# Routed feed-forward tiles: gated activations split into rounded halves ahead of the transpose, on one core

## What is computed

```python
sorted_x = xf[tok]                                   # tokens in the order of their experts
g = jax.lax.ragged_dot(sorted_x, gate_w, group_sizes)    # 512 -> 256
u = jax.lax.ragged_dot(sorted_x, up_w, group_sizes)      # 512 -> 256
h = jax.nn.silu(g) * u                               # gated activations
o = jax.lax.ragged_dot(h, down_w, group_sizes)       # 256 -> 512
o = o * w.reshape(-1)[order][:, None]
routed = jnp.zeros_like(xf).at[tok].add(o)
```

## Time and profile before

| | |
|---|---|
| median of three timed runs | 3971.14 us (3970.76 to 3972.11) |
| span of the profiled execution | 4018.9 us |
| TensorE matmuls busy | 3900.7 us, 97% of the span |
| ScalarE, VectorE, POOL busy | 1510.2, 1695.7, 1923.6 us |
| mean granted TensorE clock | 0.985 of full speed |
| routed stage, first matmul at | 1467.03 us |

### The profile page before, as it was taken

How to read it: one execution, slowest core, us unless ns; L and a number is a source line. 1 busy time by engine, 2 the same in 40 slices (tenths; PEclk the granted TensorE clock), 3 DMA queues, 4 the chain that set the end, 5 groups by cost and what they waited for, 6 DMA issues and landing times.

```text
span 4018.9 us, 92670 instructions
## 1 busy us (share of the span) xinstructions
PE 3900.7 (97%) x19160; PEld 3193.3 (79%) x19161; DVE 1695.7 (42%) x4076; ACT 1510.2 (38%) x3339; POOL 1923.6 (48%) x1598
## 2 busy tenths in 40 slices
PE   6999999999999969999999999999999999999998
PEld 5877777877777858888888888888888888888886
DVE  4655555555555533333333333333333333333343
ACT  3222222222222214444444444444444444444444
POOL 1353333333333425555555555555555555555554
PEclk7999999999999989999999999999999999999999
DMA  5121122121112126666676676767666776777776
GB/s 178 48 59 43 43 54 54 43 57 50 43 51 48 41 64 111 112 139 115 110 141 114 111 141 111 143 112 140 112 141 112 142 143 110 142 141 144 141 141 128
DMA packets 296940, 409.20 MB, mean 102 GB/s; under 512 B 116137, under 2 KB 151345, under 8 KB 296817
## 3 DMA queue, kind: packets, MB, share of 16 engines
q0 software_dynamic: 135872, 280.60, 37.8%
q1 hardware_dynamic: 160946, 127.03, 12.9%
HBM read 228.29 MB, written 179.19 MB: 101 GB/s over the span
## 4 chain that ended last, share of the span: by engine, by line
PE 62%; issue 1%; ACTq 0%; DMA 0%; ACT 0%; DVEq 0%; DVE 0%; SPq 0%; POOL 0%; POOLq 0%
PE bank L1229 37%; PE bank L1247 18%; PE bank L1220 4%; PE bank L1238 3%; ACTq L1325 0%; DMA raw_gu<-in_L_ffn_up_w_dram 0%; DVE w_dn_l L30 0%; DMA trow<-tile_table 0%; ACT w_gu_h L1317 0%; DVEq L1076 0%; POOL out_dram L1182 0%; SPq L1065 0%; ACTq L1065 0%; ACT x_h L1291 0%; ACT w_dn_h L1317 0%
## 5 line engine op out<-in xcount | busy, mean ns | idle before, releaser
L1182 POOL DMA_INDIRECT out_dram<-o_rows,to_row x532 | 862.1, 1620 | 970.0 <-issue 783.9
L422 POOL DMA_INDIRECT slot_list<-ent,pos x512 | 504.7, 986 | 874.8 <-PE bank L448 389.0
L1395 DVE TENSOR_TENSOR e_hf<-bank,e_sg 128x256 f32<-128x256 f32 x532 | 225.7, 424 | 1595.6 <-issue 808.6
L1229 PE MATMUL bank<-w_gu_h,x_h 128*128 x2128 | 842.9, 396 | 7.8 <-DVE x_l L30 5.1
L1229 PE MATMUL bank<-w_gu_l,x_h 128*128 x2128 | 840.9, 395 | 0.0
L1229 PE MATMUL bank<-w_gu_h,x_l 128*128 x2128 | 839.7, 395 | 0.0
L1166 POOL DMA_INDIRECT x_rows<-y_rows,from_row x536 | 537.6, 1003 | 215.1 <-issue 129.0
L1297 ACT ACTIVATE e_sg<-bank 128x256 f32<-128x256 f32 x532 | 204.3, 384 | 863.8 <-PE bank L1229 672.8
L1229 PEld LDWEIGHTS bank<-w_gu_h,x_h 128*128 128x128 f32 x2128 | 401.1, 188 | 109.8 <-issue 16.4
L1229 PEld LDWEIGHTS bank<-w_gu_h,x_l 128*128 128x128 f32 x2128 | 401.5, 189 | 94.2
L1229 PEld LDWEIGHTS bank<-w_gu_l,x_h 128*128 128x128 f32 x2128 | 401.2, 189 | 92.3
(11 more groups left out here) (244 smaller groups left out, 6022.8 us busy)
## 6 DMA issues: line engine op xcount, KB each, us to landing
xin<-in_x_dram SPq DMA_DIRECT2D x16, 1024.0 KB
y_rows<-yrow SPq DMA_DIRECT2D x64, 256.0 KB
stage_d<-in_x_dram SPq DMA_DIRECT2D x16, 1024.0 KB
out_dram<-stage_d SPq DMA_DIRECT2D x16, 1024.0 KB
raw_gu<-in_L_ffn_gate_w_dram SPq DMA_DIRECT2D x29, 512.0 KB
raw_gu<-in_L_ffn_up_w_dram SPq DMA_DIRECT2D x29, 512.0 KB
raw_d<-in_L_ffn_down_w_dram SPq DMA_DIRECT2D x29, 512.0 KB
lists<-slot_list SPq DMA_DIRECT2D x538, 1.0 KB
```

The lines of the kernel that those rows point to most:

```text
L422: nc.gpsimd.indirect_dma_start(slots, bass.IndirectOffsetOnAxis(ap=pos[v][:, t, k:k + 1], axis=0), ent[v][:, t, k, :], None).then_inc(scat ...
L1182: nc.gpsimd.indirect_dma_start(out, bass.IndirectOffsetOnAxis(ap=to_row[u][:].bitcast(U32), axis=0), og[u][:], None, compute_op=ALU.add).t ...
L1229: last = nc.tensor.matmul(b_gu[u % 2][:], xp[a][:, u % 2, k, :], wgu[b][:, bass.ds(place, 1), k, :].rearrange("p a n -> p (a n)"), start=( ...
L1395: nc.vector.tensor_tensor(hf[:, u % 2, :], b_gu[u % 2][:, H:2 * H], sg[:, u % 2, :], ALU.mult).then_inc(dve_gu, 1)
```

## The change

`e_hf` is no longer transposed itself. ScalarE rounds it into a high half `e_r_h` (`h_round`), VectorE subtracts that from `e_hf` into a low half `e_r_l` (`h_rest`), both of 128 x 256 in SBUF. `turn_h` transposes the two halves as float32r with `ident_r`, four transposes into all 512 columns of the bank, and waits for `dve_hr`, the low half. Behind it `h_high` still copies the first 256 columns to SBUF, and `h_low` copies the last 256 with a plain copy where it subtracted. In the order of the steps `h_round` stands between `x_high` and `h_high`, `h_rest` between `x_low` and `rows_from`. The wait for the turn of two tiles before moves from the product to the two new operations.

```diff
--- before.py
+++ after.py
@@ -1033,6 +1033,7 @@
             sg = sb("e_sg", [P, 2, H])
             hf = sb("e_hf", [P, 2, H])
             ident_r = sb("ident_r", [P, P], F32R)
+            hr = [sb("e_r_h", [P, 2, H], F32R), sb("e_r_l", [P, 2, H], F32R)]
             hp = [sb("e_h_h", [P, 2, KH, P], F32R), sb("e_h_l", [P, 2, KH, P], F32R)]
             og = [sb(f"o_rows{n}", [P, C]) for n in range(UN)]
 
@@ -1050,6 +1051,7 @@
             words, words_chain, ident_ok = sem("words"), sem("words_chain"), sem("ident_ok")
             pe_x, act_x, dve_x = sem("pe_x"), sem("act_x"), sem("dve_x")
             pe_gu, act_gu, dve_gu = sem("pe_gu"), sem("act_gu"), sem("dve_gu")
+            act_hr, dve_hr = sem("act_hr"), sem("dve_hr")
             pe_ht, act_ht, dve_ht = sem("pe_ht"), sem("act_ht"), sem("dve_ht")
             pe_do = sem("pe_do")
             act_do = sem("act_do")
@@ -1233,9 +1235,11 @@
 
                 def turn_h(j, u):
 
-                    pe.wait_ge(dve_gu, j + 1)
-                    for k in range(KH):
-                        last = nc.tensor.transpose(b_h[u % 2][:, k * P:(k + 1) * P], hf[:, u % 2, k * P:(k + 1) * P], ident[:])
+                    pe.wait_ge(dve_hr, j + 1)
+                    for a in range(2):
+                        for k in range(KH):
+                            last = nc.tensor.transpose(b_h[u % 2][:, a * H + k * P:a * H + (k + 1) * P].bitcast(F32R),
+                                                       hr[a][:, u % 2, k * P:(k + 1) * P], ident_r[:])
                     last.then_inc(pe_ht, 1)
 
                 def down(j, u, place):
@@ -1296,6 +1300,12 @@
                         act.wait_ge(dve_gu, j - 1)
                     nc.scalar.activation(sg[:, u % 2, :], b_gu[u % 2][:, 0:H], ACT.Silu).then_inc(act_gu, 1)
 
+                def h_round(j, u):
+                    act.wait_ge(dve_gu, j + 1)
+                    if not isinstance(j, int) or j >= 2:
+                        act.wait_ge(pe_ht, j - 1)
+                    nc.scalar.copy(hr[0][:, u % 2, :], hf[:, u % 2, :]).then_inc(act_hr, 1)
+
                 def h_high(j, u):
                     act.wait_ge(pe_ht, j + 1)
                     if not isinstance(j, int) or j >= 2:
@@ -1340,6 +1350,7 @@
                         start_weights(j + 2, turn.order(u + 2))
                     silu(j, u)
                     x_high(j + 2, (u + 2) % UN)
+                    h_round(j, u)
                     if not known or j >= 1:
                         h_high(j - 1, (u - 1) % UN)
                     with act.If(turn.first(u + 2) > 0):
@@ -1390,14 +1401,18 @@
 
                 def hidden(j, u):
                     dve.wait_ge(act_gu, j + 1)
+                    nc.vector.tensor_tensor(hf[:, u % 2, :], b_gu[u % 2][:, H:2 * H], sg[:, u % 2, :], ALU.mult).then_inc(dve_gu, 1)
+
+                def h_rest(j, u):
+                    dve.wait_ge(act_hr, j + 1)
                     if not isinstance(j, int) or j >= 2:
                         dve.wait_ge(pe_ht, j - 1)
-                    nc.vector.tensor_tensor(hf[:, u % 2, :], b_gu[u % 2][:, H:2 * H], sg[:, u % 2, :], ALU.mult).then_inc(dve_gu, 1)
+                    sub_exact(nc, hr[1][:, u % 2, :], hf[:, u % 2, :], hr[0][:, u % 2, :]).then_inc(dve_hr, 1)
 
                 def h_low(j, u):
                     dve.wait_ge(act_ht, j + 1)
-                    sub_exact(nc, hp[1][:, u % 2, :, :].rearrange("p k t -> p (k t)"), b_h[u % 2][:, 0:H],
-                              hp[0][:, u % 2, :, :].rearrange("p k t -> p (k t)")).then_inc(dve_ht, 1)
+                    nc.vector.tensor_copy(hp[1][:, u % 2, :, :].rearrange("p k t -> p (k t)"),
+                                          b_h[u % 2][:, H:2 * H]).then_inc(dve_ht, 1)
 
                 def weights_low(order, parts):
 
@@ -1416,6 +1431,7 @@
                         weights_low(turn.order(u + 1), (1, 2))
                     hidden(j, u)
                     x_low(j + 2, (u + 2) % UN)
+                    h_rest(j, u)
                     rows_from(j + 2 + UN, (u + 2) % UN, g + 2 if u >= UN - 2 else g + 1)
                     if not isinstance(j, int) or j >= 1:
                         h_low(j - 1, (u - 1) % UN)
```

## The result

The changed kernel takes 4075.74 us (median of 4 runs, 4070.72 to 4077.93); the kernel before, beside it, 3971.62 us. The ratio is 1.0259, with a 95% interval of 1.0246 to 1.0271: 104 us slower. The forecast was 4059 us, in a range of 3996 to 4096.

A forecast was written before the change was run, and what follows sets the result against it. TensorE was taken to bound the routed stage, 532 steps of 4.71 us. Turns +85 us and expert changes +3 us gave +88 us on the median 3971.14: 4059 us, range 3996 to 4096.

The forecast's parts named there:

- The bound: Routed stage: TensorE's chain of 532 steps of 4.71 us; other engines' work counts only where TensorE waits for it.
- The price of a turn: TensorE, each step: seven rounded turns at 0.083 us and an eighth at 0.11, +0.16 a step, +85 us.
- the block: TensorE's x and h turns in one routed step, forecast to take 0.69 us with eight rounded turns.
- e: Interval of the eighth rounded turn, with a down product's weight load under it: taken as 0.11 us, between 0.06 and 0.17.
- flat rate: Rival, TensorE turns: every rounded turn costs 0.073 us, +0.05 a step, +27 us, 3998 us; chance 0.11.
- short turns: Rival: the added four turns and the x turn ahead take 0.06 us or less, +0.02 a step, 3982 us; chance 0.05.
- faster: Rival: eight rounded turns fall under 0.53 us; at 0.06 each, -0.05 a step, -27 us, 3944 us; chance 0.03.
- What the chain would show: Changed profile: 8 turns of 0.69 to 0.75 us, a 4.87 us step, products unchanged at 2.79 and 1.40.
- ScalarE and VectorE in ordinary steps: Added 0.40 us on ScalarE and 0.42 on VectorE a step cost nothing; some 2 us of cover remain.
- The 48 us between the profiled span and the median: Profiled span 4018.9 us against median 3971.14, place unknown; the forecast difference was added to the median as it stood.
- Where an expert changes, the cover is thin: At 28 weight loads VectorE's +0.42 us lands on the chain: +0.1 us each, +3 us, ends -2 and +12.
- a sign of being wrong: Changed profile: more than a few us of the difference lying outside the four TensorE lines.

The follow-up runs named there:

- TensorE's part alone: Kernel before with four rounded turns of h in place of two plain ones, nothing added on ScalarE or VectorE: 4092.61 us beside 4007.89, ratio 1.0212.
- the first experiment: Kernel before with two rounded turns of h in place of the two plain ones, nothing else changed: 4008.03 us beside 4007.89, ratio 1.0001.
- The wait alone: Kernel before with ScalarE's wait for VectorE's product added, carried by an empty instruction, without the copy: ratio 1.0043, +16.9 us.
- both operations at the old speed: Kernel before with ScalarE's rounding copy and VectorE's subtraction added, results unused, the two plain turns kept: ratio 1.0057, +21.3 us.
- the copy alone: Kernel before with ScalarE's added copy of e_hf and its wait for VectorE's product, result unused: ratio 1.0055, +21.1 us.

## Why the prediction was right, and where it was not

**The bound.** Right. TensorE was and stayed the chain in ordinary steps, and 85 of 104 us come with the four turns alone. Every step's gain or loss on TensorE went through.

**The price of a turn.** Right, and it is most of the result: +0.16 a step and +85 us was forecast for the block, and the starts of the loads give +0.168, 89 us. That TensorE's part alone measured +84.7, so near to 85, is partly luck, since a few us of stops saved are in it. The seven intervals put at 0.083 were 0.086, and e, taken as 0.11 between 0.06 and 0.17, was 0.108. The rivals by which a rounded turn costs less (flat rate, short turns, faster) fall with the first experiment: two rounded turns cost what two plain ones do. The Trainium skill ("TensorE: Matmul & The Clock Gate", Weight-path perf modes) gives a fast weight load to 128 weights of a type other than FP32. No trace here shows one for float32r: the load of either kind takes 0.14 us, and the rounded one takes longer to be followed.

**What the chain would show.** Wrong in the place. The turns were to take 0.69 to 0.75 us there; they take 0.29 + 0.34, and 0.07 to 0.08 us appear in the down products, which I had said would stay.

**ScalarE and VectorE in ordinary steps.** Right: 0.407 and 0.415 us were measured for 0.40 and 0.42, the plain copy costs 0.414 like the subtraction that it replaced, and TensorE never waits for the new subtraction. The 48 us between the profiled span and the median, added as they stood, did no harm either: 44 of them lay in the first stage.

**The step that failed** is "Where an expert changes, the cover is thin": +3 us, with an upper end of 12, where the stops grew by 12 to 15, and where the other engines' work added 19 us to the four turns alone. VectorE's own share was sized well (+3.5 in stops by itself, +5.5 timed). What was left out is ScalarE. The prediction looked at the wait that the change gives ScalarE in an ordinary step only, where the product is done in time, and named the h copy as the work behind it. At a change of expert VectorE splits weights before it makes the product, so the wait is 1.3 us in the mean, and behind it stand the result rows and the next casts, on which VectorE's next split hangs, on which TensorE hangs; at the change shown above the next set's first cast came 2.5 us later than before. The wait alone brings +13.3 us of stops and the copy +5.5; the 0.32 us more that TensorE takes over two steps gives back part (27.1 us of stops with both operations at the old speed, 19.9 in the changed kernel). It is also why the present waits grew to 1.6 us and did not, as said, stay under 0.6. The prediction had named this as a sign of being wrong: more than a few us outside the four TensorE lines. The forecast stayed inside its range because the block, where it was right, is so much larger: of the 17 us by which it was too low, 1 to 4 are the block and 12 to 9 the stops, by the two splits above, and the rest lies outside the stretch between the silus.

**What stays open.** That a late cast makes a late split and a late TensorE is read from the order of the work at one change and from the wait lists; no run delays the casts alone. How the copy's share divides between its place and its length isn't settled by +5.5 and +2.2 us, and no run tells the added wait from the empty instruction that carries it. With the copy alone and with the wait alone ScalarE waited at 73 and 72 places, 38.8 and 37.3 us in all, and in the changed kernel at 25, 33.7 us; the many short waits of the two were not followed up.

## What to carry to other kernels

Price a short matmul by the load that stands under it, and read it from the starts of the weight loads, not from the ends in the chain; then the order of unlike short matmuls is something to try, worth 10 us here for no work. Where two engines hand work to each other, look at a new wait in the busiest step and not in the ordinary one: one added wait, with no work of its own, on an engine that was 44% busy cost 13 us of stops, and moving the copy that waits to the end of its engine's step cost 30 us more, because the engine it served then waited in turn.

## What the runs showed that had not been expected

A rounded transpose of 128 x 128 with the load of another rounded one under it takes 0.085 us, with that of a plain one 0.06, although both loads are recorded with 0.14. A plain transpose takes 0.11 with a plain, a rounded or a product's load under it. At the granted clock of 1.00, the upper level of 2.4 GHz, a rounded transpose with a product's float32r load under it takes 0.108; at 0.50, the level of 1.2 GHz, it was 0.17.
